# A two-layer graph attention kernel on one Trainium2 core: every engine's list of calls in a new order

## Chip, cores and metric

One NeuronCore of a Trainium2 chip runs the whole kernel. The metric is device time in microseconds from the first to the last instruction with what lies around them, median of several runs. PE is TensorE, DVE VectorE, ACT ScalarE, POOL GpSimd, SP the queue that issues the transfers.

## What is computed

Two layers act on 128 graphs of 128 nodes with 256 features. Both attend over nodes under the graph's adjacency; the second has a norm ahead of it and an MLP of 1024 hidden units behind it.

```python
# layer 0, for each graph (x: 128 x 256, adj: 128 x 128, 8 heads of 32)
q, k, v = x @ Wq + bq, x @ Wk + bk, x @ Wv + bv
attn = softmax(where(adj == 0, -inf, q @ k.T / sqrt(32)))
y = (attn @ v) @ Wo + bo + x
x = (y - mean(y)) * rsqrt(var(y) + eps) * gamma + beta
# layer 1
nx = layernorm(x) * ln1_g + ln1_b
q, k, v = nx @ wq + bq, nx @ wk + bk, nx @ wv + bv
attn = softmax(q @ k.T / sqrt(32) + where(adj > 0, 0.1 * adj * adj, -inf))
x1 = x + (attn @ v) @ wo + bo
out = x1 + gelu((layernorm(x1) * ln2_g + ln2_b) @ w1 + b1) @ w2 + b2
```

## The kernel before

Graphs go in 32 batches of four (G = 4), so a tile holds 4 x 128 rows. Each operand of a product is kept as a high part and a low part (hi on ScalarE, lo on VectorE), and a product is three matmuls (high-high, high-low, low-high) into one PSUM bank. A batch passes these jobs of TensorE, each a bank filled: QKV0 0 to 5, S0 (scores), F0 (transposes of the softmax), V0 (values), WO0 (output projection), T1 0 and 1 (transposes of the normalised rows), the same again for layer 1 (QKV1, S1, F1, V1, WO1), T2 0 and 1, MLP1 0 to 7 and MLP2. X and Y stand for layer 0 and layer 1 in the calls.

Four stages of four different batches are under way at once. Each engine has one function `body(i)`, a list of calls written out by hand or by a planner, in which `i`, `i - 1`, `i - 2`, `i - 3` are the batches of the stages. The order of the calls is the order of the engine's queue; nothing overtakes. `iterate` runs it for i from -1 to 34: the rounds 5 to 30 are a hardware loop (26 rounds, 25 jumps back), the others are unrolled.

JOBS gives each job of a round its place in PE's order, how many rounds its batch is behind, and its bank (0 to 7). From this table `filled` and `taken` work out the semaphore values: `filled` waits until PE has filled a job's bank, `taken` until its reader has emptied it, and `open_job` makes PE wait until the bank's last use was emptied.

The steps that the text follows:

- `norm_stats(2)`, `root(2)` (POOL, a power), `norm_rows(2)` (DVE, L802, four instructions of 128 x 256 from x1 to r1), then PE's `flip_rows("T2")` (L406) transposes r1, ACT copies the high part and DVE's `lo("T2")` (L736) the low part; `mlp_up(0)` (L395) waits for that.
- `scores(Y, 0)` (L362) waits for the two `pad_k(Y)` of POOL (L869, 128 x 1024 from hf), which wait for DVE's `qk_lo` (L755).
- `recip` (DVE, L717) releases `normalise` (POOL, L861, in place in pm), whose result `flip` (L375) transposes; `copy_pt` (DVE half: L722) takes the transposes away. `mask_scores` (L702) writes the scores of the next group into the same half of pm, so it waits for the flip (`flipped`).
- `values` (L388) gives V, `out_hi` (ACT) and `out_lo` (DVE, L729) split it, `out_proj` (L395, weights wo) uses it.
- `split_h` (DVE L810, POOL L914) subtracts the high part of the gelu's result; even parts are on DVE, odd parts on POOL.

Of the kernel before, what the change touches and what calls it, by code (L numbers as in the profile page):

```python
# [84 lines left out]
def program(nc, x, xT, adj, w):  # L85
    ctx = ExitStack()
    with ctx:
# [219 lines left out]
        def _(pe):  # L307
# [7 lines left out]
            bias = ps[2]  # L315
# [147 lines left out]
            def body(i):  # L463
                qkv(X, i, 0); flip(Y, i - 2, 0, 1); scores(Y, i - 2, 2); scores(Y, i - 2, 3); qkv(X, i, 1)
                qkv(X, i, 2); mlp_down(i - 3, 0); flip(Y, i - 2, 1, 0); qkv(X, i, 3); flip(Y, i - 2, 1, 1)
                qkv(X, i, 4); mlp_down(i - 3, 1); mlp_down(i - 3, 2); values(Y, i - 2, 0); scores(X, i, 0)
# [15 lines left out]
        def _(sc):  # L482
# [112 lines left out]
            def body(i):  # L595
                copy_pt(X, i - 1, 2); hi("T2", i - 3, 0); hi("T2", i - 3, 1); out_hi(X, i - 1, 0); exp(Y, i - 2, 0, 0)
                copy_pt(X, i - 1, 3); exp(Y, i - 2, 0, 1); gelu(i - 3, 0); gelu(i - 3, 1); gelu(i - 3, 2)
                gelu(i - 3, 3); gelu(i - 3, 4); out_hi(X, i - 1, 1); gelu(i - 3, 5); x_hi(i, 0); x_hi(i, 1)
                gelu(i - 3, 6); gelu(i - 3, 7); exp(Y, i - 2, 1, 0); qk_hi_out(X, i, 0); exp(Y, i - 2, 1, 1)
                copy_pt(Y, i - 2, 0); qk_hi_out(X, i, 1); qk_hi_out(X, i, 2); qk_hi_out(X, i, 3); copy_pt(Y, i - 2, 1)  # L600
                exp(Y, i - 2, 2, 0); exp(Y, i - 2, 2, 1); exp(Y, i - 2, 3, 0); exp(Y, i - 2, 3, 1)
                copy_pt(Y, i - 2, 2); out_hi(Y, i - 2, 0); exp(X, i, 0, 0); exp(X, i, 0, 1); copy_pt(Y, i - 2, 3)
# [362 lines left out]
```

## Time and profile before

| | |
|---|---|
| median of 3 runs | 2283.95 us (2281.99 to 2287.57) |
| the profiled execution | 2286.4 us, its span 2284.5 us |
| PE busy | 2163.5 us, 95% of the span, 19008 matmuls |
| DVE busy | 1929.0 us, 84% |
| ACT busy | 1828.2 us, 80% |
| POOL busy | 1429.4 us, 63% |
| chain that ended last | PE 85%, DVE 10%, issue 2%, ACT 2%, POOL 1% |
| DMA | 73.79 MB, 32 GB/s over the span |
| granted TensorE clock, mean | 0.980 |

Busy is time with an instruction under way; for PE the ends of matmuls are modelled, so its starts are the better measure. A wait is put down to the instruction whose end came last before it.

### The profile page before, as it was taken

Reading aid. Unit: us, or ns where it says so; the run is one execution under the profiler, and the core shown is the slowest. Engines: PE = TensorE matmul, PEld = TensorE weight load, DVE = VectorE, ACT = ScalarE, POOL = GpSimd, SP = SyncE. Lnnn points to the kernel's source line nnn. Section 1 sums busy time; section 2 is a strip of 40 time slices with the busy share of each in tenths; the row PEclk is TensorE's granted clock in tenths of the full one; section 3 lists DMA queues with packets and bytes.
Section 4 is the critical chain, followed back from the end, with each engine's and each line's share of the span. In section 5 each row is a group of like instructions: output and inputs, shape, how many; then the busy total and the mean of one; then the engine's idle time right before and its main releaser. Section 6 shows DMA issues by size and latency. Waiting matters only on the chain.

```text
span 2284.5 us, 59848 instructions
## 1 busy us (share of the span) xinstructions
PE 2163.5 (95%) x19008; PEld 1908.8 (84%) x19008; DVE 1929.0 (84%) x7045; ACT 1828.2 (80%) x5774; POOL 1429.4 (63%) x1037
## 2 busy tenths in 40 slices
PE   6789999999999999999999999999999999999987
PEld 5678888888888888888888888888888888888876
DVE  5889888889888889888889888889888889888862
ACT  4688888878888888888888888888888888888863
POOL 2566676666676666666566676666666666666642
PEclk8899999999999999999999999999999999999998
DMA  4101101101101101101101100101110101110000
GB/s 127 31 27 38 34 15 38 37 28 37 33 14 37 37 28 37 33 17 34 37 28 37 33 24 28 37 28 37 33 33 19 37 28 37 33 37 6 25 10 19
DMA packets 80891, 73.79 MB, mean 32 GB/s; under 512 B 3008, under 2 KB 72256, under 8 KB 80704
## 3 DMA queue, kind: packets, MB, share of 16 engines
q1 hardware_dynamic: 80704, 71.98, 10.8%
q14 instruction: 153, 1.25, 0.2%
q8 instruction: 34, 0.56, 0.1%
HBM read 55.20 MB, written 16.78 MB: 32 GB/s over the span
## 4 chain that ended last, share of the span: by engine, by line
PE 85%; DVE 10%; issue 2%; ACT 2%; POOL 1%; DMA 0%; SPq 0%; DVEq 0%; POOLq 0%
PE ps L395 58%; PE ps L375 10%; PE ps L362 9%; DVE r L802 4%; PE ps L388 4%; PE ps L406 3%; DVE pm L702 2%; DVE hf L755 1%; ACT pm L515 1%; POOL pm L861 0%; DVE nmax L702 0%; PE ps L335 0%; DVE stats L787 0%; DMA m<-in_adj 0%; DVE xy L802 0%
## 5 line engine op out<-in xcount | busy, mean ns | idle before, releaser
L515 ACT ACTIVATE pm<-pm,nmax 128x128 f32<-128x128 f32 x2048 | 794.1, 394 | 76.4 <-DVE nmax L702 74.4
L861 POOL TENSOR_TENSOR pm<-pm,rinv 128x512 f32<-128x512 f32 x512 | 529.7, 1050 | 407.0 <-DVE rinv L717 407.0
L702 DVE CUSTOM_DVE_ANT_0 pm<-ps,m 128x128 f32<-128x128 f32 x2048 | 461.2, 284 | 45.4 <-PE ps L362 27.0
L515 ACT ACTIVATION_READ_ACCUMULATOR pm<-pm,nmax 128x1 f32 x2048 | 393.2, 192 | 0.0
L375 PE MATMUL ps<-ident,pm 128*128 128x128 f32 x2048 | 291.3, 278 | 11.0 <-POOL pm L861 9.9
L395 PE MATMUL ps<-w2h,hh 128*128 128x256 f32 x1024 | 290.9, 284 | 2.8 <-issue 2.8
L914 POOL TENSOR_TENSOR hl<-hf,hh 128x512 fp32r<-128x512 f32 x128 | 168.0, 1313 | 195.1 <-ACT hf L592 195.1
L395 PE MATMUL ps<-w2h,hl 128*128 128x256 f32 x1024 | 288.1, 281 | 0.0
L395 PE MATMUL ps<-w2l,hh 128*128 128x256 f32 x1024 | 288.0, 281 | 0.0
L375 PEld LDWEIGHTS ps<-ident,pm 128*128 128x128 f32 x2048 | 231.8, 141 | 47.0 <-POOL pm L861 14.5
L523 ACT ACTIVATE pt<-ps 128x512 f32<-128x512 f32 x256 | 151.3, 591 | 100.9 <-PE ps L375 100.9
L395 PE MATMUL ps<-acth,w1h 128*128 128x512 f32 x512 | 209.8, 410 | 2.1 <-DVE actl L736 2.1
L395 PE MATMUL ps<-acth,w1l 128*128 128x512 f32 x512 | 203.7, 398 | 0.0
L395 PE MATMUL ps<-actl,w1h 128*128 128x512 f32 x512 | 203.4, 397 | 0.0
L395 PEld LDWEIGHTS ps<-w2h,hh 128*128 128x128 f32 x1024 | 193.8, 189 | 4.8 <-issue 3.2
L876 POOL TENSOR_TENSOR rstd<-veps,power 128x4 f32<-128x4 f32 x96 | 97.5, 1016 | 157.7 <-DVE veps L795 154.5
L395 PEld LDWEIGHTS ps<-w2l,hh 128*128 128x128 f32 x1024 | 193.8, 189 | 1.2
L395 PEld LDWEIGHTS ps<-w2h,hl 128*128 128x128 f32 x1024 | 193.8, 189 | 0.0
L722 DVE COPY pt<-ps 128x512 f32<-128x512 f32 x256 | 172.5, 684 | 14.2 <-PE ps L375 14.2
L586 ACT ACTIVATE hh<-ps,b 128x512 fp32r<-128x512 f32 x256 | 179.8, 702 | 4.8 <-PE ps L395 2.9
L810 DVE TENSOR_TENSOR hl<-hf,hh 128x512 fp32r<-128x512 f32 x128 | 93.0, 727 | 106.8 <-ACT hf L592 55.3
L592 ACT ACTIVATE hf<-ps,b 128x512 f32<-128x512 f32 x256 | 181.0, 707 | 0.0
(149 smaller groups left out, 6631.7 us busy)
## 6 DMA issues: line engine op xcount, KB each, us to landing
xTr<-in_xT SPq DMA_DIRECT2D x32, 512.0 KB, 3.7
xy<-in_x SPq DMA_DIRECT2D x32, 512.0 KB, 5.0
out<-x SPq DMA_DIRECT2D x32, 512.0 KB, 3.4
m<-in_adj SPq DMA_DIRECT2D x32, 256.0 KB, 2.8
a<-in_adj SPq DMA_DIRECT2D x32, 256.0 KB, 5.3
r<-in_wo SPq DMA_DIRECT2D x2, 256.0 KB, 6.5
x<-in_w SPq DMA_DIRECT2D x1, 512.0 KB, 8.6
v<-in_w SPq DMA_DIRECT2D x1, 512.0 KB, 7.2
```

What stands on the lines that cost most here:

```text
L362: last = mm(outs[c][:, pair_of].rearrange("p (h n) -> p h n", h=2), q[l][hq][rows, k, gs], kp[l][hk][rows, k, :, gs], start=(t == 0), stop ...
L375: last = nc.tensor.transpose(out[:, j * N:(j + 1) * N], pm[:, g % 2, c * HC + j, :], ident[:, :])
L395: last = mm(out, pick(parts[a], c), wpick(wparts[b], c), start=(n == 0), stop=(n == len(terms) - 1))
L515: last = nc.scalar.activation(pm[:, g % 2, h, :], pm[:, g % 2, h, :], ACT.Exp, bias=nmax[:, g % 2, h:h + 1], scale=-1.0, accum_out=rsum[:, ...
L523: nc.scalar.activation(pt[:, g % 2, 0:HC, :], src[:, :].rearrange("p (h q) -> p h q", h=HC), ACT.Copy).then_inc(free_of(f"F{l}", 2 * g), 1)
L586: nc.scalar.activation(hh[0][:, m, :], src[:, :], ACT.Gelu, bias=b1[:, m:m + 1])\
L592: nc.scalar.activation(hf[:, m % 2, :], src[:, :], ACT.Gelu, bias=b1[:, m:m + 1])\
L702: last = nc.vector.tensor_tensor_reduce(out=pm[:, g % 2, h, :], in0=src[:, j * N:(j + 1) * N], in1=m[:, g, :], scale=1.0, scalar=3e38, op0 ...
L722: nc.vector.tensor_copy(pt[:, g % 2, HC:H, :], src[:, :].rearrange("p (h q) -> p h q", h=HC))\
L861: tt(pm[:, g % 2, hs, :], pm[:, g % 2, hs, :], rinv[:, g % 2, hs].rearrange("p (h a) -> p h a", a=1).to_broadcast([P, HC, N]), ALU.mult).t ...
L876: tt(rstd[:, k, :], veps[:, k, :], power[:, :], ALU.pow).then_inc(rstd_done[k], 1)
L914: tt(hh[1][:, m, :], hf[:, m % 2, :], hh[0][:, m, :].bitcast(F32), ALU.subtract).then_inc(h_lo[1], 1)
```

## The change

The lists of calls of PE, ACT, DVE and POOL are replaced by others with the same calls. Each list also begins at another call than before, so the end of the loop's body lies elsewhere on each engine: on DVE it lay between `recip(Y, 0)` and `split_h(0)` and now lies between `mask_scores(X, 2, 0)` and `out_lo(Y, 1)`; on PE it lay behind F1 0 and now lies between MLP1 3 and MLP1 4. JOBS has the new order, batches behind and banks. `taken_all` waits once for each bank where `values` waited for each job. The bias products of the start use bank 3 in place of 2. Odd parts of h stay on POOL. SP's list is unchanged.

```diff
--- before.py
+++ after.py
 JOBS = [
-    ("QKV0", 0, 0, 1), ("F1", 1, 2, 5), ("S1", 4, 2, 7), ("S1", 5, 2, 3), ("S1", 6, 2, 6), ("S1", 7, 2, 2),
-    ("QKV0", 1, 0, 0), ("QKV0", 2, 0, 5), ("MLP2", 0, 3, 1), ("F1", 2, 2, 7), ("QKV0", 3, 0, 4), ("F1", 3, 2, 0),
...
+    ("MLP1", 4, 3, 1), ("MLP1", 5, 3, 7), ("MLP1", 6, 3, 3), ("MLP1", 7, 3, 5), ("WO0", 0, 1, 1), ("WO0", 1, 1, 7),
+    ("S1", 4, 2, 2), ("S1", 5, 2, 3), ("S1", 6, 2, 6), ("S1", 7, 2, 4), ("F1", 0, 2, 5), ("QKV0", 0, 0, 7),
...
+        def taken_all(eng, b, out, jobs):
+
+            last = {}
+            for job in sorted(jobs, key=lambda job: (BEHIND[POS[job]], POS[job])):
+                last[BANK[POS[job]]] = job
+            last.pop(BANK[POS[out]], None)
+            for name, n in last.values():
+                taken(eng, b, name, n)
+
...
             def values(l, b, half):
                 if exists(b):
-                    if half == 0:
-                        taken(pe, b, f"QKV{l}", 5)
                     out = open_job(b, f"V{l}", half)
                     for g in (2 * half, 2 * half + 1):
-                        taken(pe, b, f"F{l}", 2 * g)
-                        taken(pe, b, f"F{l}", 2 * g + 1)
+                        v_read = [(f"QKV{l}", 5)] if g == 0 else []
+                        taken_all(pe, b, (f"V{l}", half), v_read + [(f"F{l}", 2 * g), (f"F{l}", 2 * g + 1)])
                         for h in range(H):
...
-                qkv(X, i, 0); flip(Y, i - 2, 0, 1); scores(Y, i - 2, 2); scores(Y, i - 2, 3); qkv(X, i, 1)
-                qkv(X, i, 2); mlp_down(i - 3, 0); flip(Y, i - 2, 1, 0); qkv(X, i, 3); flip(Y, i - 2, 1, 1)
-                qkv(X, i, 4); mlp_down(i - 3, 1); mlp_down(i - 3, 2); values(Y, i - 2, 0); scores(X, i, 0)
-                scores(X, i, 1); flip(Y, i - 2, 2, 0); flip(Y, i - 2, 2, 1); mlp_down(i - 3, 3); qkv(X, i, 5)
-                flip(Y, i - 2, 3, 0); flip(Y, i - 2, 3, 1); flip_rows("T1", i - 1, 0); flip_rows("T1", i - 1, 1)
-                out_proj(Y, i - 2, 0); values(Y, i - 2, 1); scores(X, i, 2); flip(X, i, 0, 0); flip(X, i, 0, 1)
-                qkv(Y, i - 1, 0); out_proj(Y, i - 2, 1); qkv(Y, i - 1, 1); qkv(Y, i - 1, 2); flip(X, i, 1, 0)
-                flip(X, i, 1, 1); qkv(Y, i - 1, 3); scores(X, i, 3); values(X, i, 0); qkv(Y, i - 1, 4)
-                qkv(Y, i - 1, 5); flip(X, i, 2, 0); flip_rows("T2", i - 2, 0); flip_rows("T2", i - 2, 1)
-                scores(Y, i - 1, 0); scores(Y, i - 1, 1); flip(X, i, 2, 1); flip(X, i, 3, 0); flip(X, i, 3, 1)
-                mlp_up(i - 2, 0); mlp_up(i - 2, 1); mlp_up(i - 2, 2); mlp_up(i - 2, 3); mlp_up(i - 2, 4)
-                mlp_up(i - 2, 5); values(X, i, 1); mlp_up(i - 2, 6); mlp_up(i - 2, 7); out_proj(X, i, 0)
-                out_proj(X, i, 1); flip(Y, i - 1, 0, 0)
+                mlp_up(i - 3, 4); mlp_up(i - 3, 5); mlp_up(i - 3, 6); mlp_up(i - 3, 7); out_proj(X, i - 1, 0)
+                out_proj(X, i - 1, 1); scores(Y, i - 2, 2); scores(Y, i - 2, 3); flip(Y, i - 2, 0, 0); qkv(X, i, 0)
+                qkv(X, i, 1); qkv(X, i, 2); qkv(X, i, 3); mlp_down(i - 3, 0); flip(Y, i - 2, 0, 1); mlp_down(i - 3, 1)
+                flip(Y, i - 2, 1, 0); flip(Y, i - 2, 1, 1); qkv(X, i, 4); mlp_down(i - 3, 2); scores(X, i, 0)
+                scores(X, i, 1); values(Y, i - 2, 0); flip(Y, i - 2, 2, 0); flip(Y, i - 2, 2, 1); mlp_down(i - 3, 3)
+                flip(Y, i - 2, 3, 0); qkv(X, i, 5); flip(Y, i - 2, 3, 1); flip_rows("T1", i - 1, 0)
+                flip_rows("T1", i - 1, 1); scores(X, i, 2); values(Y, i - 2, 1); flip(X, i, 0, 0); flip(X, i, 0, 1)
+                out_proj(Y, i - 2, 0); out_proj(Y, i - 2, 1); qkv(Y, i - 1, 0); qkv(Y, i - 1, 1); flip(X, i, 1, 0)
+                qkv(Y, i - 1, 2); flip(X, i, 1, 1); qkv(Y, i - 1, 3); scores(X, i, 3); values(X, i, 0)
+                qkv(Y, i - 1, 4); qkv(Y, i - 1, 5); flip_rows("T2", i - 2, 0); flip(X, i, 2, 0)
+                flip_rows("T2", i - 2, 1); scores(Y, i - 1, 0); scores(Y, i - 1, 1); flip(X, i, 2, 1)
+                flip(X, i, 3, 0); mlp_up(i - 2, 0); flip(X, i, 3, 1); mlp_up(i - 2, 1); mlp_up(i - 2, 2)
+                values(X, i, 1); mlp_up(i - 2, 3)
...
-                copy_pt(X, i - 1, 2); hi("T2", i - 3, 0); hi("T2", i - 3, 1); out_hi(X, i - 1, 0); exp(Y, i - 2, 0, 0)
-                copy_pt(X, i - 1, 3); exp(Y, i - 2, 0, 1); gelu(i - 3, 0); gelu(i - 3, 1); gelu(i - 3, 2)
...
+                exp(Y, i - 2, 3, 1); copy_pt(Y, i - 2, 2); out_hi(Y, i - 2, 0); exp(X, i, 0, 0); copy_pt(Y, i - 2, 3)
+                exp(X, i, 0, 1); hi("T1", i - 1, 0); hi("T1", i - 1, 1); exp(X, i, 1, 0); out_hi(Y, i - 2, 1)
+                exp(X, i, 1, 1); copy_pt(X, i, 0); exp(X, i, 2, 0); qk_hi_out(Y, i - 1, 0); exp(X, i, 2, 1)
+                qk_hi_out(Y, i - 1, 1); copy_pt(X, i, 1); qk_hi_out(Y, i - 1, 2); qk_hi_out(Y, i - 1, 3)
+                exp(X, i, 3, 0); exp(X, i, 3, 1); hi("T2", i - 2, 0); hi("T2", i - 2, 1); copy_pt(X, i, 2)
+                out_hi(X, i, 0); exp(Y, i - 1, 0, 0); copy_pt(X, i, 3); exp(Y, i - 1, 0, 1); gelu(i - 2, 0)
+                gelu(i - 2, 1); gelu(i - 2, 2); out_hi(X, i, 1); gelu(i - 2, 3); gelu(i - 2, 4); gelu(i - 2, 5)
+                gelu(i - 2, 6); x_hi(i + 1, 0); x_hi(i + 1, 1); gelu(i - 2, 7); exp(Y, i - 1, 1, 0)
+                exp(Y, i - 1, 1, 1); qk_hi_out(X, i + 1, 0); exp(Y, i - 1, 2, 0); qk_hi_out(X, i + 1, 1)
+                qk_hi_out(X, i + 1, 2); qk_hi_out(X, i + 1, 3); copy_pt(Y, i - 1, 0); exp(Y, i - 1, 2, 1)
...
-                split_h(i - 3, 0); split_h(i - 3, 2); mask0(i); out_lo(X, i - 1, 1); split_h(i - 3, 4); x_lo(i, 0)
-                x_lo(i, 1); residual("WO0", i - 1, 0); split_h(i - 3, 6); residual("WO0", i - 1, 1)
-                norm_stats(0, i - 1); copy_pt(Y, i - 2, 0); qk_lo(X, i, 0); mask_scores(Y, i - 2, 2, 0)
-                recip(Y, i - 2, 1); norm_rows(0, i - 1); qk_lo(X, i, 1); mask_scores(Y, i - 2, 2, 1)
-                flipped(Y, i - 2, 1, 0); mask_scores(Y, i - 2, 3, 0); qk_lo(X, i, 2); flipped(Y, i - 2, 1, 1)
-                mask_scores(Y, i - 2, 3, 1); copy_pt(Y, i - 2, 1); v_out(X, i, 0); qk_lo(X, i, 3); mask1(i - 1)
-                recip(Y, i - 2, 2); residual("MLP2", i - 3, 0); norm_stats(1, i - 1); recip(Y, i - 2, 3)
-                flipped(Y, i - 2, 2, 0); mask_scores(X, i, 0, 0); copy_pt(Y, i - 2, 2); flipped(Y, i - 2, 2, 1)
-                mask_scores(X, i, 0, 1); norm_rows(1, i - 1); out_lo(Y, i - 2, 0); residual("MLP2", i - 3, 1)
-                flipped(Y, i - 2, 3, 0); mask_scores(X, i, 1, 0); copy_pt(Y, i - 2, 3); recip(X, i, 0)
-                lo("T1", i - 1, 0); flipped(Y, i - 2, 3, 1); mask_scores(X, i, 1, 1); v_out(X, i, 1)
-                lo("T1", i - 1, 1); out_lo(Y, i - 2, 1); flipped(X, i, 0, 0); mask_scores(X, i, 2, 0); recip(X, i, 1)
-                flipped(X, i, 0, 1); mask_scores(X, i, 2, 1); residual("WO1", i - 2, 0); copy_pt(X, i, 0)
-                residual("WO1", i - 2, 1); qk_lo(Y, i - 1, 0); norm_stats(2, i - 2); copy_pt(X, i, 1)
-                qk_lo(Y, i - 1, 1); recip(X, i, 2); qk_lo(Y, i - 1, 2); mask_scores(X, i, 3, 0)
-                mask_scores(X, i, 3, 1); qk_lo(Y, i - 1, 3); norm_rows(2, i - 2); v_out(Y, i - 1, 0); recip(X, i, 3)
-                v_out(Y, i - 1, 1); lo("T2", i - 2, 0); mask_scores(Y, i - 1, 0, 0); lo("T2", i - 2, 1)
-                out_lo(X, i, 0); flipped(X, i, 2, 1); mask_scores(Y, i - 1, 0, 1); copy_pt(X, i, 2); copy_pt(X, i, 3)
-                flipped(X, i, 3, 0); mask_scores(Y, i - 1, 1, 0); flipped(X, i, 3, 1); mask_scores(Y, i - 1, 1, 1)
-                recip(Y, i - 1, 0)
+                out_lo(Y, i - 3, 1); lo("T1", i - 2, 1); recip(X, i - 1, 1); flipped(X, i - 1, 0, 1)
+                mask_scores(X, i - 1, 2, 1); residual("WO1", i - 3, 0); residual("WO1", i - 3, 1)
+                copy_pt(X, i - 1, 0); norm_stats(2, i - 3); qk_lo(Y, i - 2, 0); copy_pt(X, i - 1, 1)
+                recip(X, i - 1, 2); norm_rows(2, i - 3); qk_lo(Y, i - 2, 1); qk_lo(Y, i - 2, 2)
+                mask_scores(X, i - 1, 3, 0); qk_lo(Y, i - 2, 3); mask_scores(X, i - 1, 3, 1); v_out(Y, i - 2, 0)
+                v_out(Y, i - 2, 1); recip(X, i - 1, 3); lo("T2", i - 3, 0); mask_scores(Y, i - 2, 0, 0)
+                lo("T2", i - 3, 1); out_lo(X, i - 1, 0); flipped(X, i - 1, 2, 1); mask_scores(Y, i - 2, 0, 1)
+                copy_pt(X, i - 1, 2); copy_pt(X, i - 1, 3); flipped(X, i - 1, 3, 0); mask_scores(Y, i - 2, 1, 0)
+                flipped(X, i - 1, 3, 1); mask_scores(Y, i - 2, 1, 1); recip(Y, i - 2, 0); split_h(i - 3, 0); mask0(i)
+                out_lo(X, i - 1, 1); split_h(i - 3, 2); split_h(i - 3, 4); split_h(i - 3, 6); x_lo(i, 0); x_lo(i, 1)
+                residual("WO0", i - 1, 0); residual("WO0", i - 1, 1); norm_stats(0, i - 1); flipped(Y, i - 2, 0, 0)
+                mask_scores(Y, i - 2, 2, 0); recip(Y, i - 2, 1); qk_lo(X, i, 0); norm_rows(0, i - 1); qk_lo(X, i, 1)
+                qk_lo(X, i, 2); flipped(Y, i - 2, 0, 1); mask_scores(Y, i - 2, 2, 1); copy_pt(Y, i - 2, 0)
+                qk_lo(X, i, 3); flipped(Y, i - 2, 1, 0); mask_scores(Y, i - 2, 3, 0); recip(Y, i - 2, 2)
+                flipped(Y, i - 2, 1, 1); mask_scores(Y, i - 2, 3, 1); v_out(X, i, 0); copy_pt(Y, i - 2, 1)
+                residual("MLP2", i - 3, 0); norm_stats(1, i - 1); mask1(i - 1); recip(Y, i - 2, 3)
+                flipped(Y, i - 2, 2, 0); mask_scores(X, i, 0, 0); out_lo(Y, i - 2, 0); copy_pt(Y, i - 2, 2)
+                flipped(Y, i - 2, 2, 1); mask_scores(X, i, 0, 1); residual("MLP2", i - 3, 1); norm_rows(1, i - 1)
+                flipped(Y, i - 2, 3, 0); mask_scores(X, i, 1, 0); recip(X, i, 0); copy_pt(Y, i - 2, 3)
+                flipped(Y, i - 2, 3, 1); mask_scores(X, i, 1, 1); lo("T1", i - 1, 0); v_out(X, i, 1)
+                flipped(X, i, 0, 0); mask_scores(X, i, 2, 0)
...
-                pad_k(Y, i - 2, 3); normalise(X, i - 1, 2, 1); normalise(X, i - 1, 3, 0); normalise(X, i - 1, 3, 1)
-                add_b2(i - 3); add_bo0(i - 1); normalise(Y, i - 2, 0, 0); split_h(i - 3, 1); split_h(i - 3, 3)
-                normalise(Y, i - 2, 0, 1); split_h(i - 3, 5); split_h(i - 3, 7); add_bo1(i - 2); root(0, i - 1)
-                normalise(Y, i - 2, 1, 0); normalise(Y, i - 2, 1, 1); scale_y0(i - 1); pad_k(X, i, 2); shift_y0(i - 1)
-                pad_k(X, i, 3); normalise(Y, i - 2, 2, 0); normalise(Y, i - 2, 2, 1); root(1, i - 1)
-                normalise(Y, i - 2, 3, 0); normalise(Y, i - 2, 3, 1); normalise(X, i, 0, 0); normalise(X, i, 0, 1)
-                normalise(X, i, 1, 0); normalise(X, i, 1, 1); root(2, i - 2); normalise(X, i, 2, 0)
-                pad_k(Y, i - 1, 2)
+                root(0, i - 1); normalise(Y, i - 2, 1, 0); normalise(Y, i - 2, 1, 1); scale_y0(i - 1); pad_k(X, i, 2)
+                shift_y0(i - 1); pad_k(X, i, 3); normalise(Y, i - 2, 2, 0); normalise(Y, i - 2, 2, 1)
+                normalise(Y, i - 2, 3, 0); root(1, i - 1); normalise(Y, i - 2, 3, 1); normalise(X, i, 0, 0)
+                normalise(X, i, 0, 1); normalise(X, i, 1, 0); normalise(X, i, 1, 1); add_bo0(i); root(2, i - 2)
+                normalise(X, i, 2, 0); pad_k(Y, i - 1, 2); pad_k(Y, i - 1, 3); normalise(X, i, 2, 1)
+                normalise(X, i, 3, 0); normalise(X, i, 3, 1); add_bo1(i - 1); add_b2(i - 2); normalise(Y, i - 1, 0, 0)
+                split_h(i - 2, 1); split_h(i - 2, 3); split_h(i - 2, 5); split_h(i - 2, 7); normalise(Y, i - 1, 0, 1)
```

## Rows read from the trace of the kernel before

**Rows 1.** PE's waits over twenty rounds, 568.5 to 1926.7: us, times, longest
```profile
PE ps L406 <- DVE r L802: 37.3, 20, 1.9
```

**Rows 2.** Timeline, all engines: start us, duration, engine, instruction, [idle before]
```profile
1042.95 3.67 DVE L802 TENSOR_SCALAR r<-x,mv,rstd 128x256 f32<-128x256 f32 x4
...
1043.12 2.00 POOL L869 TENSOR_TENSOR kp1l<-hf,pair 128x1024 fp32r<-128x1024 f32 x1 [0.55 <-DVE hf L755]
...
1044.30 0.60 PE L375 MATMUL ps<-ident,pm 128*128 128x128 f32 x4
...
1046.76 1.09 PE L406 MATMUL ps<-ident,r 128*128 128x128 f32 x8 [1.86 <-DVE r L802]
...
1114.68 1.91 PE L406 MATMUL ps<-ident,r 128*128 128x128 f32 x8 [1.87 <-DVE r L802]
```

**Rows 3.** Waits of DVE's split_h over the whole span
```profile
DVE hl L810 <- ACT hh L586: 51.5, 25, 2.3
```

**Rows 4.** Timeline at split_h, one unrolled and one looped round
```profile
236.65 0.69 DVE L810 TENSOR_TENSOR hl<-hf,hh 128x512 fp32r<-128x512 f32 x1 [1.38 <-ACT hf L592]
...
1053.42 0.18 ACT L515 ACTIVATION_READ_ACCUMULATOR pm<-pm,nmax 128x1 f32 x1
...
1054.71 0.20 DVE L717 RECIPROCAL rinv<-rsum 128x8 f32<-128x8 f32 x1
...
1055.50 0.68 ACT L592 ACTIVATE hf<-ps,b 128x512 f32<-128x512 f32 x1
...
1057.02 0.69 DVE L810 TENSOR_TENSOR hl<-hf,hh 128x512 fp32r<-128x512 f32 x1 [2.10 <-ACT hh L586]
```

**Rows 5.** DMA queue of instructions, 700 to 1500 and 1054.78 to 1055.5: packets, MB
```profile
q14 instruction: 59, 0.48, 0.2%
...
q14 instruction: 1, 0.01, 4.8%
```

**Rows 6.** Timeline around F0 0 and the mask behind it
```profile
1098.38 0.68 DVE L729 TENSOR_TENSOR otl<-ps,oth 128x512 fp32r<-128x512 f32 x1
...
1098.43 1.09 PE L375 MATMUL ps<-ident,pm 128*128 128x128 f32 x8
...
1099.37 0.29 DVE L702 CUSTOM_DVE_ANT_0 pm<-ps,m 128x128 f32<-128x128 f32 x1 [0.30 <-PE ps L375]
```

**Rows 7.** PE's timeline from QKV1 3 to MLP1 0
```profile
1037.85 0.48 PE L395 MATMUL ps<-acth,wqkv1h 128*128 128x512 f32 x1
...
1041.35 0.38 PE L395 MATMUL ps<-wqkv1h,acth 128*128 128x256 f32 x1
...
1047.78 0.39 PE L362 MATMUL ps<-kp1h,q1h 64*128 64x256 f32 x2
...
1049.40 1.53 PE L375 MATMUL ps<-ident,pm 128*128 128x128 f32 x12
...
1050.69 0.48 PE L395 MATMUL ps<-acth,w1h 128*128 128x512 f32 x1
```

**Rows 8.** norm_rows beside GpSimd (first two rows) and alone
```profile
1072.73 2.78 DVE L802 TENSOR_SCALAR xy<-xy,mv,rstd 128x256 f32<-128x256 f32 x4
...
1072.89 2.15 POOL L861 TENSOR_TENSOR pm<-pm,rinv 128x512 f32<-128x512 f32 x2 [1.19 <-DVE rinv L717]
...
1091.55 1.57 DVE L802 TENSOR_SCALAR xy<-y,mv,rstd 128x256 f32<-128x256 f32 x4
```

**Rows 9.** Timeline of DVE and POOL behind QKV1 3 and behind T2
```profile
1038.13 0.69 DVE L722 COPY pt<-ps 128x512 f32<-128x512 f32 x1 [0.28 <-PE ps L375]
...
1040.67 1.90 POOL L869 TENSOR_TENSOR kp1l<-hf,pair 128x1024 fp32r<-128x1024 f32 x1
...
1048.94 0.29 DVE L702 CUSTOM_DVE_ANT_0 pm<-ps,m 128x128 f32<-128x128 f32 x1 [0.17 <-PE ps L362]
...
1049.79 0.69 DVE L736 TENSOR_TENSOR actl<-ps,acth 128x512 fp32r<-128x512 f32 x1
```

**Rows 10.** Groups by form, whole span: xcount, busy us, mean ns
```profile
L755 DVE SCALAR_TENSOR_TENSOR hf<-ps,bk,hf 128x512 f32<-128x512 f32 x128 | 94.0, 734 | 5.6 <-ACT hf L560 5.5
```

More of the change, by code:

```diff
@@ L313, in first_weights @@
                 pe.wait_ge(lo_made, 2 * C)
-            bias = ps[2]
+            bias = ps[3]
             def shift_products():
@@ L595, in body @@
             def body(i):
-                copy_pt(X, i - 1, 2); hi("T2", i - 3, 0); hi("T2", i - 3, 1); out_hi(X, i - 1, 0); exp(Y, i - 2, 0, 0)
-                copy_pt(X, i - 1, 3); exp(Y, i - 2, 0, 1); gelu(i - 3, 0); gelu(i - 3, 1); gelu(i - 3, 2)
[L598 to L602, printed above, removed]
-                hi("T1", i - 1, 0); hi("T1", i - 1, 1); exp(X, i, 1, 0); out_hi(Y, i - 2, 1); exp(X, i, 1, 1)
-                copy_pt(X, i, 0); exp(X, i, 2, 0); qk_hi_out(Y, i - 1, 0); exp(X, i, 2, 1); qk_hi_out(Y, i - 1, 1)
-                qk_hi_out(Y, i - 1, 2); copy_pt(X, i, 1); qk_hi_out(Y, i - 1, 3); exp(X, i, 3, 0); exp(X, i, 3, 1)
+                exp(Y, i - 2, 3, 1); copy_pt(Y, i - 2, 2); out_hi(Y, i - 2, 0); exp(X, i, 0, 0); copy_pt(Y, i - 2, 3)
[8 more added lines that the diff above has]
+                qk_hi_out(X, i + 1, 2); qk_hi_out(X, i + 1, 3); copy_pt(Y, i - 1, 0); exp(Y, i - 1, 2, 1)
+                copy_pt(Y, i - 1, 1); exp(Y, i - 1, 3, 0)
             iterate(sc, body, {FIRST: before_first})
@@ L646, in second_weights @@
                 dve.wait_ge(bias_mm, 1)
-                bias = ps[2]
+                bias = ps[3]
                 tt(bo[0][:, :], bo[0][:, :], bias[:, D:2 * D], ALU.add).then_inc(bias_step, 1)
@@ L664, in third_weights @@
                 dve.wait_ge(bias_mm, 2)
-                bias = ps[2]
+                bias = ps[3]
                 tt(b1[:, :], b1raw, bias[:, 0:FC], ALU.add).then_inc(bias_step, 1)
```

18 rows, old and new, of the table JOBS are left out of this document.

## The prediction

> **What bounds the kernel now.** I read the page first: by the shares in the table above TensorE's queue is the line on which time is counted. Then the waits of PE in twenty undisturbed rounds of the loop (568.5 to 1926.7 us). One wait repeats there: the first T2 transpose waits for the normalised r1, once a round, 1.9 us each [rows 1]. The timeline of one round gives its size on PE's own clock: the four transposes of F0 4 start at 1044.30 and take about 0.44, so T2 could start at 1044.74; it starts at 1046.76, 2.0 us late [rows 2]. The same rows say why. norm_rows(2), four DVE instructions from SBUF to SBUF, takes 3.67 us beside GpSimd's pad_k, where the same form takes 1.57 with GpSimd idle [rows 2, 8]. The wait ends again at 1114.68, so a round is 67.9 us; without it PE's work and its small gaps are 65.9.
>
> So the most that a new order can give is about 2.0 us a round. Over 32 batches that is 64 us.
>
> **The change part by part.** No arithmetic is added or taken out. The number of instructions is the same, the odd parts of h stay on GpSimd, and taken_all only merges waits on a bank. PE's blocks keep their lengths: an F block alone or beside others costs 0.11 a transpose [rows 7], and the runs of scores and values have as many edges as before. I cost this at nothing. All of the change lies in where waits end, so I follow PE's new order and put beside each block the shortest chain that starts on PE and comes back to it. Most blocks have 0.5 us or more to spare. Four places count.
>
> *T2.* norm_rows(2) now stands ahead of qk_lo(Y,1), two masks and two qk_lo, and T2 0 follows QKV1 5 directly. From QKV1 3's start PE needs 1044.30 - 1037.85 = 6.45 us to reach it [rows 2, 7]. The chain starts from F0 3, which ends as QKV1 3 starts: copy_pt 0.28 after that start [rows 7, 9], 0.6 for it, 0.1 for the reciprocal, norm_rows at most 3.7. It is done by 4.7. The wait goes: -2.0.
>
> *WO1 1.* PE now does F0 0, F0 1, WO1 0, WO1 1 in a row. From F0 0's start that is eight transposes (0.86) and twelve 256-column matmuls; 24 of those with one entry take 1044.30 - 1041.35 = 2.95, so twelve are about 1.5 [rows 2, 7]. WO1 1 could start at +2.4. It needs out_lo(Y,1), which on DVE stands behind mask_scores(X,2,0), which needs F0 0. Today the mask starts 1099.37 - 1098.43 = 0.94 after F0 0's start [rows 6]; a mask group is 0.85 (1048.94 to 1049.79) [rows 9]; out_lo 0.68 [rows 6]; 0.1 to wake PE. That is +2.55, already 0.15 late. But between this mask and this out_lo the new DVE body is cut: the mask is the last call and out_lo the first.
>
> What the cut costs can be seen today, where it lies between recip(Y,0) and split_h(0). In the unrolled rounds split_h starts 0.1 us after ScalarE has written hf [rows 4], idle 1.38 before it and released by hf. In the looped ones DVE sits idle 2.06 us on average, 25 times [rows 3], which is the number of times the loop jumps back, and it starts late: at 1054.71 the reciprocal, hf ready at 1056.18, split_h at 1057.02 [rows 4]. A packet of instructions is fetched in the 0.7 us behind the reciprocal, and such fetches go on at five a round through the loop [rows 5]. Today gelu would keep DVE waiting 1.4 us there, so 0.6 to 0.9 of it shows, on no path of PE's. In the new order nothing covers it. Could DVE's sequencer run ahead of the mask? The reciprocal's input had been ready since 1053.6 [rows 4], and yet the fetch comes only after it has started, so I take all of it: 2.1. WO1 1 waits 0.15 + 2.1 = 2.2 us in looped rounds, 0.15 in the others. Bounds: 0.15 if the jump hides in the mask, 2.45 by the longest such idle, 2.3 [rows 3].
>
> *S1 0.* From QKV1 3's start PE needs 6.45 and then T2 0, F0 4, T2 1 (twelve transposes, 1.29 plus an entry of 0.15): scores(Y,0) could start at +7.9. They need both pad_k of Y. The chain on DVE and POOL: copy_pt at +0.28, 0.6; recip(X,2) 0.1; norm_rows(2), clear 1.57; qk_lo 1 and 2, 0.65 to the next start and 0.73 [rows 10]; 0.1; two pad_k of 1.9 [rows 9]; 0.1. Sum 7.9: just in time, if GpSimd lets norm_rows alone. But recip(X,2), the call just before it, is what releases GpSimd's normalise(X,2,0). The same pair stands today at 1072.7: norm_rows(0) starts, POOL's normalise 0.16 later, and the four take 2.78 instead of 1.57, 1.2 more [rows 8]. I take 1.2, since it is the same neighbour. Bounds: 0 if the port stays free, 2.1 by norm_rows beside pad_k (3.67 against 1.57).
>
> [...]
>
> *MLP1 0.* It needs lo(T2,1), behind mask_scores(Y,0,0). From the scores' start: mask 1.16 later, 0.85, 0.69, so 2.75 [rows 7, 9]. PE has now two scores (1.62) and two F blocks (0.86) in between, where there were three: 2.5. It waits 0.3. Bounds 0 and 0.5.
>
> The sum. A looped round changes by -2.0 + 2.2 + 1.2 + 0.3 = +1.7; 25 of them make +42. The other seven change by -2.0 + 0.15 + 1.2 + 0.3 = -0.35, together -2. Start and end of the program I leave, since the order within one batch is nearly the same. Total +40 on the profiled execution: 2286.4 (span 2284.5 and 1.9 around it) becomes 2326. That execution was 2.45 above the median of the runs, so I predict **2324 us**.
>
> **The rivals.** 0.3% is 6.9 us, about what a measurement of this kernel tells from no change.
>
> *B. The cut costs, GpSimd does not.* GpSimd's normalise could come late enough to fall behind norm_rows. A looped round changes by -2.0 + 2.2 + 0.3 = +0.5, the seven by -1.55: together 0 to +2, 2285. Against it: today's pair at 1072.7.
>
> *C. The cut is hidden, GpSimd's block stays.* -0.35 in all 32 rounds, -11: 2273. For it: the mask is four instructions and gives a sequencer something to run ahead of, which one reciprocal does not.
>
> *D. The change does what its words say, and the cut costs nothing.* -1.55 in 32 rounds is -50. The brief falls of the granted clock that some of the T2 waits are followed by would go too: about 2230. This is the other sign. It decides only if the gap after the mask is under 0.5 us and norm_rows(2) stays at 1.6.
>
> *E. More cuts or waits.* PE's cut moves to between MLP1 3 and 4, and ACT's into the exponentials of Y. If one of these showed as DVE's does, 25 times 2.1 or 52 us more: about 2375. Against it, PE's waits of twenty rounds show none at its cut today [rows 1], behind F1 0. Small waits where I saw 0.1 to 0.4 to spare (T1 0, F0 6, MLP1 1) come under this case too: 2345 to 2375.
>
> [...]
>
> **How the numbers follow.** A 0.50, B 0.15, C 0.12, D 0.10, E 0.13. A alone reaches from 2305 (the block at half its size) to 2342 (cut at 2.3 and the waits at their upper bounds in part). The range of 8 in 10 leaves out D and most of E: 2266 to 2345. Slower by over 0.3%: A, E and a quarter of B, 0.67. Within it: half of B and a little of C, 0.11. Faster: C, D and the rest, 0.22.
>
> **What would show it.** In the new profile the T2 wait is gone from PE's list. WO1 1 (wo1h, oth) waits for DVE's otl about 2 us, 25 times, and DVE is idle that long between mask and otl in the looped rounds alone. norm_rows on r takes 2.6 to 2.8 for four, not 1.6. PE waits about 1.2 us for POOL's kp1l before the scores of Y, and a round is 69.6 us. If DVE's idle stretch before otl is short, the cut was wrong; if norm_rows is 1.6, the port was; if PE waits in a place not named here, my walk along the order missed it.

## Result: 2319.7 us, 1.5% slower

The changed kernel takes 2319.7 us (median of 4 runs, 2318.26 to 2320.85), the kernel before 2284.5 in the same session: a ratio of 1.0153, interval 1.0136 to 1.0171. The prediction was 2324, range 2266 to 2345. The profiled span is 2318.9 us where it was 2284.5, so +34.4.

The page of the kernel after, its busy times, shows that no other engine became the bound by work:

```profile
PE 2183.8 (94%) x19008; PEld 1918.2 (83%) x19008; DVE 1749.9 (75%) x7045; ACT 1821.3 (79%) x5774; POOL 1403.0 (61%) x1037
```

DVE is 179 us less busy, its instructions from SBUF to SBUF above all (the four of norm_rows(2) take 2.06 us where they took 3.67), and yet the kernel is slower. The waits of PE and of DVE over twenty rounds (564.3 to 1972.8; us, times, longest) say where:

```profile
PE ps L402 <- DVE otl L737: 52.0, 20, 2.8
PE ps L402 <- DVE q1l L759: 3.4, 17, 0.2
PE ps L371 <- POOL kp1l L878: 2.9, 16, 0.2
...
DVE otl L737 <- issue: 51.4, 20, 2.8
```

The wait for r ahead of T2 [rows 1] is gone, and a larger one has come: WO1 1 waits for otl 2.6 us in each of these rounds, and DVE was idle just as long ahead of that otl, waiting for nothing that the profile shows. The timeline has the place (start, duration; idle time before in brackets):

```profile
1046.38 0.28 PE L402 MATMUL ps<-wo1h,otl 128*128 128x256 f32 x1
1049.16 0.39 PE L402 MATMUL ps<-wo1h,oth 128*128 128x256 f32 x1 [2.51 <-DVE otl L737]
...
1045.64 0.28 DVE L710 CUSTOM_DVE_ANT_0 pm<-ps,m 128x128 f32<-128x128 f32 x1
1045.86 0.08 DVE L710 DVE_READ_ACCUMULATOR2_ANT nmax<- 128x1 f32 x1
1048.42 0.69 DVE L737 TENSOR_TENSOR otl<-ps,oth 128x512 fp32r<-128x512 f32 x1 [2.48 <-issue]
```

The mask at 1045.64 is the last call of DVE's loop body and the otl at 1048.42 the first. One packet of DVE's instruction queue falls into that gap (1045.94 to 1048.42):

```profile
q14 instruction: 1, 0.01, 1.2%
```

Behind the wait the granted clock of PE falls in 16 of the 25 looped rounds. These windows (us, busy time and count of PE, PEld, DVE, ACT, POOL, then the clock, DMA share, GB/s) stand at the same place of two neighbouring rounds, 0.94 us behind the end of waits of 2.51 and 2.63 us:

```profile
1050.10:1053.50 3.40, 3.40 (x13) 2.88 (x12) 3.17 (x12) 0.00 (x0) 3.40 (x3) 0.53 0.01 2
1121.10:1124.50 3.40, 3.40 (x20) 2.80 (x19) 3.15 (x12) 1.22 (x4) 3.40 (x3) 1.00 0.01 2
```

In the first the clock is 0.50 of full speed from 1050.5 to 1053.0 us, 0.53 over the 3.4 us, and 13 matmuls were under way in it instead of 20. The start of norm_rows(2) marks each round:

```profile
215.19 2.06 DVE L810 TENSOR_SCALAR r<-x,mv,rstd 128x256 f32<-128x256 f32 x4
281.95 2.06 DVE L810 TENSOR_SCALAR r<-x,mv,rstd 128x256 f32<-128x256 f32 x4
...
987.32 2.06 DVE L810 TENSOR_SCALAR r<-x,mv,rstd 128x256 f32<-128x256 f32 x4
...
1058.23 2.06 DVE L810 TENSOR_SCALAR r<-x,mv,rstd 128x256 f32<-128x256 f32 x4
...
1127.67 2.05 DVE L810 TENSOR_SCALAR r<-x,mv,rstd 128x256 f32<-128x256 f32 x4
```

An unrolled round takes 66.76 us. A looped one takes 69.44 (1058 to 1127, no fall of the clock) or 70.91 (987 to 1058, with one at 1050). Over the whole trace 9 looped rounds are of 69.4 and 16 of 71.0. In the kernel before a round takes 67.92 whether looped or not, and 69.47 in the 7 in which the clock fell behind the T2 wait.

So the +34.4 is made up thus, over the same intervals between starts of norm_rows(2) in both kernels: the 25 with a jump in the kernel after 53.2 longer (1760.4 against 1707.2), the other four full ones 6.2 shorter, the two that run out at the end 5.6 shorter, and the first batch 7.0 us sooner at its norm_rows(2).

### The profile page after: what moved, and what is told of

The parts are those of the page before. It is cut to its first block, busy times and chain, and to the rows that moved or that the text cites. A ratio compares the mean times of both kernels' runs of the same rounds, so it can differ in the third digit from the quotient of the medians.

```text
span 2318.9 us, 59678 instructions
## 1 busy us (share of the span) xinstructions
PE 2183.8 (94%) x19008; PEld 1918.2 (83%) x19008; DVE 1749.9 (75%) x7045; ACT 1821.3 (79%) x5774; POOL 1403.0 (61%) x1037
## 4 chain that ended last, share of the span: by engine, by line
PE 85%; DVE 7%; issue 5%; ACT 2%; POOL 1%; DMA 0%; DVEq 0%; SPq 0%; POOLq 0%
PE ps L402 60%; PE ps L384 10%; PE ps L371 8%; PE ps L395 4%; PE ps L413 3%; DVE r L810 2%; DVE pm L710 1%; DVE otl L737 1%; DVE q1l L759 1%; ACT pm L522 1%; DVE pt L730 0%; DVE stats L795 0%; PE ps L344 0%; DMA m<-in_adj 0%; DVE rinv L725 0%
## 5 line engine op out<-in xcount | busy, mean ns | idle before, releaser
L710 DVE CUSTOM_DVE_ANT_0 pm<-ps,m 128x128 f32<-128x128 f32 x2048 | 466.9, 285 | 116.2 <-PE ps L384 108.8
L522 ACT ACTIVATION_READ_ACCUMULATOR pm<-pm,nmax 128x1 f32 x2048 | 388.1, 189 | 0.0
L384 PE MATMUL ps<-ident,pm 128*128 128x128 f32 x2048 | 298.1, 278 | 15.6 <-POOL pm L870 8.7
L737 DVE TENSOR_TENSOR otl<-ps,oth 128x512 fp32r<-128x512 f32 x128 | 88.1, 689 | 123.7 <-issue 64.5
```

The costliest lines, as they stand in the source:

```text
L384: last = nc.tensor.transpose(out[:, j * N:(j + 1) * N], pm[:, g % 2, c * HC + j, :], ident[:, :])
L522: last = nc.scalar.activation(pm[:, g % 2, h, :], pm[:, g % 2, h, :], ACT.Exp, bias=nmax[:, g % 2, h:h + 1], scale=-1.0, accum_out=rsum[:, ...
L710: last = nc.vector.tensor_tensor_reduce(out=pm[:, g % 2, h, :], in0=src[:, j * N:(j + 1) * N], in1=m[:, g, :], scale=1.0, scalar=3e38, op0 ...
L737: tt(ot[1][:, :, cols_h], bank_of(f"V{l}", half)[:, :].rearrange("p (c t) -> p c t", c=C), ot[0][:, :, cols_h].bitcast(F32), ALU.subtract) ...
```

## The experiments

All were timed beside the kernel before on the same chip; its medians were 2286.15 (first four), 2285.2 (next four) and 2286.31 (last four). Each edit is on DVE's loop alone.

**Is it the cut?** The first takes the order after and begins DVE's list at split_h(0), where it began before.

```
 def body(i):
-    out_lo(Y, i - 3, 1); lo("T1", i - 2, 1); ... recip(Y, i - 2, 0); split_h(i - 3, 0); ...
-    ... flipped(X, i, 0, 0); mask_scores(X, i, 2, 0)
+    split_h(i - 3, 0); mask0(i); ... mask_scores(X, i, 2, 0); out_lo(Y, i - 2, 1); ...
+    ... mask_scores(Y, i - 1, 1, 1); recip(Y, i - 1, 0)
```

> The changed order on every engine, call for call, but VectorE's list begins at split_h(0), where the list before the change began; nothing else differs. Theory A (the jump back of VectorE's loop leaves it idle about 2.5 us, and its new place puts this on the path): the wait of WO1 1 falls from 2.5 to at most 0.3 us in all rounds, a looped round takes 66.8 us as the unrolled ones of the changed kernel do, in place of 69.4, and the falls of the clock behind the wait (16 of 1.55 us) go: 2320 - 25 x 2.65 - 25 = about 2229 us. Rival 1 (WO1 1 waits because of the new order itself): no change, 2315 to 2325. Rival 2 (the gap only moves and is met at its old place too): 2265 to 2290.

Measured: 2232.26 us, ratio 0.9770 (0.9753 to 0.9786). All looped rounds are 66.77, as the unrolled ones, with no fall of the clock. The idle time still exists, and lies where gelu keeps DVE waiting anyway, away from PE's path, as in [rows 3]:

```profile
DVE hl L818 <- ACT hh L593: 70.9, 25, 3.1
```

So moving this one cut gives back 87 us of the changed kernel's time, and the new order with the cut there is 2.3% faster than the kernel before.

**The cut in the order before.** If a cut on PE's path costs 2.1 us or more, one put ahead of lo("T2", 1) should make the old kernel slow.

```
 def body(i):
-    split_h(i - 3, 0); ... lo("T2", i - 2, 0); mask_scores(Y, i - 1, 0, 0); lo("T2", i - 2, 1); ...
+    lo("T2", i - 3, 1); ... split_h(i - 3, 0); ... lo("T2", i - 2, 0); mask_scores(Y, i - 1, 0, 0)
```

> The order before the change, call for call, but VectorE's list now ends with mask_scores(Y,0,0) and begins with lo(T2,1), for which MLP1 0 waits without any time to spare; nothing else differs. Theory A: 25 looped rounds grow by 2.3 to 2.6 us each and the unrolled ones not at all: 2284.5 + 60 = about 2345, up to 2365 if more falls of the clock follow the longer wait. Rival 1 (the gap belongs to the new order or its neighbours): 2280 to 2290. Rival 2 (four mask instructions hide half of the jump): about 2315.

Measured: 2286.38 us, ratio 1.0003 (0.9994 to 1.0013). A miss. DVE's timeline shows no gap at the cut; actl starts 0.06 us after the mask's last instruction has started:

```profile
1049.38 0.29 DVE L702 CUSTOM_DVE_ANT_0 pm<-ps,m 128x128 f32<-128x128 f32 x1
1049.59 0.08 DVE L702 DVE_READ_ACCUMULATOR2_ANT nmax<- 128x1 f32 x1
1049.65 0.69 DVE L736 TENSOR_TENSOR actl<-ps,acth 128x512 fp32r<-128x512 f32 x1
```

And the queue's list has 28 instruction packets in the whole span, where the kernels before and after both have 153. The 125 missing are five in each of 25 looped rounds (first line the kernel after, second this run). Only DVE's list differs, so q14 is DVE's queue:

```profile
q14 instruction: 153, 1.25, 0.2%
...
q14 instruction: 28, 0.23, 0.0%
```

So this cut costs nothing: 2286.38 us against the 2286.15 of the kernel before. The 2.6 us stand where the 125 packets are, and here there are none.

**A hint.** In the kernel after the loop's closing branch is announced at the top of each round.

```
-            with eng.Fori(FIRST_FULL, LAST_FULL + 1) as i:
+            with nc.Fori(FIRST_FULL, LAST_FULL + 1, engines=[eng.engine], hint_back_edge=hint) as i:
...
-            iterate(dve, body, {FIRST: first_weights})
+            iterate(dve, body, {FIRST: first_weights}, hint=True)
```

**Half as many jumps.** Two rounds in one body, so 12 jumps.

```
-            with eng.Fori(FIRST_FULL, LAST_FULL + 1) as i:
+            with eng.Fori(FIRST_FULL, LAST_FULL + 1, 2 if twice else 1) as i:
                 body(i)
+                if twice:
+                    body(i + 1)
```

> The changed kernel with VectorE's loop holding two rounds in its body, so that it jumps back 12 times in place of 25; the other engines as they were. Theory A: 13 of the 25 stretches of 2.65 us go and about half of the 16 falls of the clock: 2320 - 34 - 12 = about 2273. If the cost belongs to each round and not to each jump: 2320. If a longer body costs more fetches per jump, up to 2300.

Measured: 2271.93 us (2265.36 to 2277.71), ratio 0.9952 (0.9935 to 0.9969). DVE's idle time ahead of otl is there 12 times, 2.55 us each, the others being gone; 114 packets are left:

```profile
DVE otl L739 <- issue: 30.6, 12, 2.7
```

The cost goes with the number of jumps: rounds of 69.3 to 70.8 alternate with rounds of 66.8. The clock fell in 3 of the 12 in the profiled run, which was the fastest of the four.

**Place alone.** The next three place the first instruction of DVE's loop at a given slot (`head_slot` in the edit). Order, cut and length of the body stay, and nothing is hinted. First the kernel after at slot 0, and its control at slot 100:

```
-            with eng.Fori(FIRST_FULL, LAST_FULL + 1) as i:
+            at = {} if slot is None else {"head_slot": {eng.engine: slot}}
+            with nc.Fori(FIRST_FULL, LAST_FULL + 1, engines=[eng.engine], **at) as i:
...
-            iterate(dve, body, {FIRST: first_weights})
+            iterate(dve, body, {FIRST: first_weights}, slot=0)     # the control: slot=100
```

> The kernel after, its order and its cut unchanged; alone the first instruction of VectorE's loop is placed at slot 0 of a block of the instruction store, without a hint. Theory (the jump back costs its 2.5 us only where the loop's code has to be fetched again, which its place decides): no instruction packets of VectorE's queue in the loop, no idle time ahead of out_lo(Y, 1), 2230 to 2235 us as with the hint. Rival (the jump back is always fetched, and the hint hid it in the earlier run): packets and 2.5 us of idle time remain, 2320 us.

> The kernel after with the first instruction of VectorE's loop at slot 100 of a block: the control for slot 0. [...] Rival (placing the loop at a fixed slot removes the fetch whatever the slot): 2232 us.

Measured: 2229.91 us at slot 0, ratio 0.9759 (0.9743 to 0.9775), and 2329.85 at slot 100, ratio 1.0191 (1.0174 to 1.0208). The page of slot 0 has 28 packets, the page of slot 100 153, and its waits have the gap of the kernel after:

```profile
q14 instruction: 28, 0.23, 0.0%
```

```profile
PE ps L403 <- DVE otl L738: 70.2, 27, 3.3
...
DVE otl L738 <- issue: 68.8, 26, 3.3
```

100 us lie between two programs that differ in nothing but where the loop begins. The hint isn't needed. Slot 100 came out 5 us above 2315 to 2325, the author's estimate from the kernel after (2319.7): its gap is 2.65 us where the kernel after has 2.58, and the clock fell in 19 of its looped rounds and not in 16. Now the order before with the moved cut, which had cost nothing, at slot 100:

> [...] Theory (place decides, and a fetched jump on the path costs 2.1 to 2.5 us a round): five instruction packets a round again, an idle 2.5 us ahead of lo(T2, 1), and 2330 to 2350 us. Rival (place does not decide, or the jump at this spot is hidden): 2286 us within 0.3%.

Measured: 2365.42 us, ratio 1.0349 (1.0332 to 1.0366). The packets are 153 again, and the gap stands ahead of actl, the first instruction behind the cut, and PE waits for it beside the T2 wait that it had:

```profile
DVE actl L737 <- issue: 64.1, 25, 2.8
...
PE ps L407 <- DVE r L803: 64.7, 32, 5.6
PE ps L396 <- DVE actl L737: 54.9, 27, 2.5
```

Packets, gap and wait come back together with the slot; the time is 15 us above the range expected. A looped round is mostly 71.4 to 72.2 where it was 67.92, of which the wait is 2.1. The expectation had not counted falls of the clock. There are 24 in the loop where the same cut unfetched has 7, and the mean clock is 0.969 against 0.981. With 1.55 us for each fall, 25 x 2.1 + 17 x 1.55 = 79 us, the difference of the two medians. Last, the kernel before at slot 0:

> The kernel before with the first instruction of VectorE's loop at slot 0 of a block. Theory (place alone decides whether the jump is fetched, and in the order before the fetch was hidden behind the wait for hh): no instruction packets in the loop, no change of the time, 2280 to 2287 us. Rival (the hidden fetch did cost something behind split_h): 2255 to 2275 us.

Measured: 2284.6 us, ratio 0.9996 (0.9987 to 1.0005), with 30 packets. The 25 waits of [rows 3] are gone: DVE waits 1.3 us for hf there, near the 1.4 of the unrolled rounds. One wait of 2.1 us is new, where the loop is entered. The time is the same: in the kernel before the fetches (153 packets against 30) cost nothing that shows: 2284.6 us against 2286.31.

**GpSimd beside norm_rows(2).** In the order after, with the list begun at split_h(0), the reciprocal that releases GpSimd's normalise goes behind the norm:

```
-                copy_pt(X, i, 1); recip(X, i, 2); norm_rows(2, i - 2); qk_lo(Y, i - 1, 1); ...
+                copy_pt(X, i, 1); norm_rows(2, i - 2); recip(X, i, 2); qk_lo(Y, i - 1, 1); ...
```

> The order after with VectorE's loop begun at split_h(0) (2232.3 us), and in it norm_rows(2) moved ahead of recip(X, 2), so that it starts before normalise(X, 2, 0) on GpSimd, which waits for that reciprocal. [...] Rival: the reciprocal and with it the normalise of X come 1.6 us later and GpSimd's pads behind them as much, so TensorE waits longer at S1 0: 2240 to 2260 us. [...]

Measured: 2211.29 us, ratio 0.9677 (0.9661 to 0.9693): 21 us less than without the swap, where the author had estimated 7 to 11 (25 rounds by 0.3 to 0.45 us: the norm at 1.6 us in place of 2.06, and two waits of PE of 0.2 us gone). A round goes from 66.77 to 66.17. In the kernel after the four rows run beside the normalise: 2.06 us (the row at 1058.23 above), of which the second alone takes 1.13. The same swap at slot 0 has them by themselves (second fence):

```profile
1058.51 1.13 DVE L810 TENSOR_SCALAR r<-x,mv,rstd 128x256 f32<-128x256 f32 x1
...
1058.39 1.10 POOL L870 TENSOR_TENSOR pm<-pm,rinv 128x512 f32<-128x512 f32 x1 [2.38 <-DVE rinv L725]
```

```profile
1009.79 1.37 DVE L811 TENSOR_SCALAR r<-x,mv,rstd 128x256 f32<-128x256 f32 x4
...
1011.35 1.04 POOL L871 TENSOR_TENSOR pm<-pm,rinv 128x512 f32<-128x512 f32 x1 [2.57 <-DVE rinv L726]
```

The clear time is 1.37 and not the 1.57 of [rows 8], so the neighbour cost 0.7 us. The round got 0.6 back; 0.4 of that are two waits of PE in the kernel after, 0.21 for q1l and 0.17 for kp1l, which are both gone. Where the other 0.2 lies was not traced.

**Both together.** The swap in the kernel after at slot 0, cut unchanged:

> The kernel after with VectorE's loop at slot 0 of a block (2229.9 us alone) and norm_rows(2) ahead of recip(X, 2). Theory (the two gains belong to different places of the round and add): the 21 us that the swap gave with the cut at split_h(0) come off here too, 2207 to 2212 us, no packets in the loop. Rival (the swap's gain was tied to the other cut): 2225 to 2230 us.

Measured: 2213.78 us, ratio 0.9682 (0.9669 to 0.9696). The gain is 16 us where it was 21, and the time 2 us above the range expected: the two add up to within 5 us. And the swap with the list begun at split_h(0), at slot 0:

> The kernel with the order after, VectorE's loop begun at split_h(0) and norm_rows(2) ahead of recip(X, 2) (2211.3 us), now with its loop at slot 0 of a block. Theory (a fetch in front of split_h(0) is hidden): 2207 to 2212 us, as with the other cut at slot 0. Rival (a hidden fetch still costs 0.3 us or more a round): under 2204 us.

Measured: 2211.77 us, ratio 0.9674 (0.9661 to 0.9688). Against the same kernel with its fetches (2211.29) nothing changes, so the hidden fetches cost nothing that shows here either. This is the best version, with either placement: 3.2 to 3.3% faster than the kernel before.

**The T2 step in the order before.** norm_rows(2) and its reciprocal are moved alone:

```
-                qk_lo(Y, i - 1, 1); recip(X, i, 2); qk_lo(Y, i - 1, 2); mask_scores(X, i, 3, 0)
-                mask_scores(X, i, 3, 1); qk_lo(Y, i - 1, 3); norm_rows(2, i - 2); ...
+                recip(X, i, 2); norm_rows(2, i - 2); qk_lo(Y, i - 1, 1); qk_lo(Y, i - 1, 2)
+                mask_scores(X, i, 3, 0); mask_scores(X, i, 3, 1); qk_lo(Y, i - 1, 3); ...
```

> The kernel before; alone norm_rows(2) and recip(X, 2) moved ahead of qk_lo(Y, 1), so that the norm no longer runs beside pad_k(Y, 3) but beside normalise(X, 2, 0). Theory (the T2 step of the prediction, -2.0 us a round, comes from this move of one step): the wait of TensorE for r ahead of T2 goes and 25 rounds by 1.5 to 2.0 us give 2235 to 2248 us. Rival (qk_lo(Y, 1 to 3) and the pads behind the norm now keep QKV1 4 and S1 0 waiting for 0.5 to 1 us): 2255 to 2270 us. Rival (the wait only moves): 2285 us.

Measured: 2262.7 us, ratio 0.9901 (0.9886 to 0.9916). The T2 wait went, and a round fell only from 67.92 to 67.58. PE's timeline and DVE's show what took its place, V0 0:

```profile
1031.62 1.08 PE L388 MATMUL ps<-pt,v 128*32 128x128 f32 x32 [1.63 <-issue]
...
1028.56 2.20 DVE L802 TENSOR_SCALAR r<-x,mv,rstd 128x256 f32<-128x256 f32 x4
1030.69 0.74 DVE L751 SCALAR_TENSOR_TENSOR q1l<-ps,nbq,q1h 128x512 fp32r<-128x512 f32 x1
```

The profile names no releaser for this wait. By the table V0 0 fills bank 0, which held QKV1 1, and that is emptied by the qk_lo(Y,1) at 1030.69, now behind the norm; it ends at 1031.43, 0.2 us before V0 0 starts. The time lies in the middle range expected, in another place than it said. No fall of the clock is left (7 before), which gives 7 x 1.55 = 11 of the 24 us. In the changed kernel V0 0 has bank 3, so its new table of banks keeps this wait away; that was not tried by itself.

## Why the prediction held, and where its sizes were off

The direction, the place and the mechanism that decides, the jump on PE's path at WO1 1, came out as case A said. Case A's second mechanism, GpSimd's block, is there at half its size. That the sum came within 5 us is luck in part: two errors of about 40 us cancel. Against the working:

- **T2, -2.0.** The wait is gone and none stands in its place. With the fetch removed and the swap made, a round without any wait of PE between 1000 and 1075 us is 66.2, against 67.92 - 1.86 = 66.06 in the kernel before [rows 2]. The term is right within 0.3.
- **WO1 1, +2.2.** The wait comes 25 times, only behind a jump, and was the largest term, as said. Its 0.15 for the order didn't show (without the fetch the wait isn't there). The fetch was put at 2.1 from [rows 3], with 2.3 as its longest; it is 2.64 by rounds (69.41 - 66.77), above that bound. What stands ahead of the cut doesn't explain the shorter gap of [rows 3]: with the new order and the same reciprocal ahead of the same split_h the idle time is 2.84 us (70.9 in 25), against 2.06 there. Why it differs no run tells. Case C's guess, that the mask might hide some of it, is refuted. What the prediction had no term for is the clock: 16 falls by 1.55 us each, where the kernel before has 7. In all the fetched jump costs 2319.7 - 2229.9 = 90 us, 3.6 a looped round.
- **"Nothing covers it."** True, but the cost is no property of a cut. The prediction took it that a loop's jump is always fetched, since it was in the trace at hand. With the head at slot 0 it is not (28 packets, 2229.9 us), at slot 100 it is (153 packets, 2329.85): here the place of the head decides it. With the loop at slot 0 the result is case D's 2230, though not for case D's reasons alone: it wanted norm_rows(2) at 1.6 us, which was 2.06.
- **S1 0, +1.2.** Overstated: PE waits 0.2 there, and norm_rows(2) takes 2.06 where 2.6 to 2.8 was the sign. The neighbour cost 0.7 and not 1.2, since [rows 8] compares a norm beside two normalises and here there was one; the swap shows that the round loses 0.6. Of what PE visibly waits, only half stands at S1 0. The other half falls on QKV1 4, which fills bank 2 behind QKV1 1 and waits for qk_lo(Y,1): a wait that the walk along the order missed. The DVE instruction that meets a normalise of 1.10 us takes 1.13; 0.40 of that it takes anyway, so the cost is 0.7. The prediction speaks of a port. No trace shows one: what they show is that an instruction of norm_rows beside one of GpSimd's lasts as long as that one. The clear time was misread too. The norm at 1091.55 is not alone: a normalise runs until 1092.00, and the first instruction of the norm takes 0.59 where the others take 0.40, so 1.57 is 1.37 and 0.2 of block. And the 3.67 of [rows 2] stand beside a pad and, from 1045.07, a normalise (kernel before, single instructions of the four):

```profile
1043.27 1.99 DVE L802 TENSOR_SCALAR r<-x,mv,rstd 128x256 f32<-128x256 f32 x1
...
1045.07 1.08 POOL L861 TENSOR_TENSOR pm<-pm,rinv 128x512 f32<-128x512 f32 x1
...
1045.18 1.12 DVE L802 TENSOR_SCALAR r<-x,mv,rstd 128x256 f32<-128x256 f32 x1
...
1090.96 1.04 POOL L861 TENSOR_TENSOR pm<-pm,rinv 128x512 f32<-128x512 f32 x1
...
1091.55 0.59 DVE L802 TENSOR_SCALAR xy<-y,mv,rstd 128x256 f32<-128x256 f32 x1
```

- **MLP1 0, +0.3.** No wait shows there.
- **The other rounds, -0.35.** They gained 1.16 (67.92 to 66.76): 0.15 less for WO1 1, 0.6 less for S1 0 and 0.3 less for MLP1 0 than was counted, against 0.3 by which T2 fell short; that is 0.75 of the 0.8.
- **Start and end, 0.** They gave -7.0 and -5.6. These were not taken apart by any run.
- **Case E.** No cut but DVE's shows in PE's waits. Beside q14 the profiles have one more queue of instructions, q8, with 34 packets in the whole span in every run, so the only packets that come round by round are q14's (153 in the span or 28), and those only with DVE's head at some places.

The cancelled errors: the fetched jump was undersized by 38 us in all (2.1 x 25 = 52 against 90), and everything else was undersized as a gain by 44 (-11 against -55). In the profiled executions at slot 0 and before, those 44 are some 22 from the rounds, 13 from start and end and 11 from the 7 falls of the clock that are gone.

What stays open: at which slots between 0 and 100 the loop is still not fetched, where the heads of the two timed kernels lie, whether the hint does anything where the body is fetched in spite of its place, and why the clock falls behind some of these waits and not behind others.

## What to carry to other kernels

Before an order is judged, look whether the instruction queue has packets in every round of a loop: if it has, a new order can gain or lose by where its code comes to lie (here 2229.9 or 2329.85 us, 4.5%), and the loop's head should be placed (or the list begun where the engine waits anyway) in both kernels. A rotated loop body is a change of its own, to be costed at the engine's first instruction behind the jump: begun at split_h(0) in place of out_lo(Y, 1), the same order took 2232.3 us in place of 2319.7. A norm from SBUF to SBUF should start before the call that releases GpSimd, which gave 16 to 21 us here, and the operations that empty banks should be walked as well as those that make data.

## What the runs showed of the hardware

- With q14's packets in the loop (153 in the span, or 114 with two rounds in the body), DVE is idle 2.55 to 2.65 us on average at a jump back where it has nothing else to wait for (the kernel after, two rounds in the body, the two at slot 100). Without packets in the loop, the kernel after has 0.2 us of such idle time ahead of otl in the whole span at slot 0 and 0.8 with the hint, and in the order before with the cut moved actl starts 0.06 us after the mask's last instruction has started. The same program with its loop's first instruction at slot 0 or slot 100 took 2229.9 or 2329.85 us.
- In the kernel after, whose PE waits 2.6 us a round, a fall of the clock followed in 16 of 25 looped rounds (to 0.53 over 3.4 us in the one shown), and with two rounds in the body behind 3 of 12 such waits; in the kernel before, with 1.9 us, in 7; in the kernel with T2 moved alone, with 1.6 us, in none. Each fall costs the round 1.55 us more.
- The four instructions of norm_rows(2) take 1.37 us alone, 2.06 beside one normalise on GpSimd, 3.67 beside a pad and a normalise [rows 2]. The one that meets a GpSimd instruction takes about as long as that: 1.13 us beside 1.10, 1.99 beside 2.00, in place of 0.40.
